# Expert layer of a four-block transformer chain: from all eight experts on every token to tokens sorted by expert, two jobs at a time

## The chip, the cores and the metric

The kernel runs on one core of a Trainium2 chip. The metric is the device time of one execution in microseconds (us). The kernel before takes 533.73 us, the median of three runs (532.73 to 534.79).

## What is computed

The input x is 16 sequences of 128 tokens with 128 features; a context of 16 sequences of 77 tokens goes with it. Four residual blocks follow each other: a cross attention without projections (A), a 16-head self attention whose projection matrices are mixed per sequence from 4 experts (B), a 16-head cross attention with rotary embedding (C), and a causal 16-head self attention that ends in a mixture of experts (D). Only the last one is touched by the change:

```python
y = x + layernorm(attn, ln1_g, ln1_b)
flat = y.reshape(-1, d)
logits = flat @ gate_W                      # 8 experts
topv, topi = jax.lax.top_k(logits, K)       # K = 2
w = jax.nn.softmax(topv, axis=-1)
combine = jnp.sum(jax.nn.one_hot(topi, E) * w[..., None], axis=1)
h = jax.nn.relu(jnp.einsum('nd,edf->enf', flat, W1) + b1[:, None, :])   # 128 -> 512
eo = jnp.einsum('enf,efd->end', h, W2) + b2[:, None, :]                 # 512 -> 128
moe = jnp.einsum('ne,end->nd', combine, eo)
out = y + layernorm(moe.reshape(b, t, d), ln2_g, ln2_b)
```

All eight experts are evaluated for every token in the formula, but only the two with the largest gate logits have a weight that isn't zero.

## The kernel before

Two sequences (`SPS = 2`, 256 tokens, `W`) are one job; there are 8 jobs. Four lanes run side by side, lane s taking jobs s and s + 4. A lane is a list of 68 small steps (`way`): transposes, projections, scores, exponentials, normalisations of the blocks A to D, up to the gate. A fifth lane (`MOE = 4`) takes the jobs in turn through the experts: `moe_start`, 16 pieces `moe` (`PIECES`), `moe_end`, `moe_out`, `store`. A sixth (`PRE = 5`) splits W1 into two half-precision parts in 8 steps.

All engines walk through the same list `STEPS`, which comes from the string `ORDER` (one digit for the lane of each of the 712 steps). Each engine does in this order what is its part of a step, and waits there on semaphores; nothing overtakes on an engine. `TAKEN` gives the PSUM bank of each step. The digits 0 to 3 of job 0's first pass reach its gate (`top`, step 194 of the list, the 187th of the lane steps) before the first digit 4 (step 200).

A `moe` piece on TensorE is two hidden blocks of 128 rows. Each is three half-precision matmuls of 256 columns (lines 659 to 661: W1hi with yhi, W1hi with ylo, W1lo with yhi), then ScalarE's relu with bias (line 804) into `hT`, and with a delay of one piece the second layer in fp32 (line 611: two token blocks for each of two hidden blocks). After each expert VectorE adds the result times the token's weight to `acc` (`take_up`, line 934). `moe_start` puts the combination with b2 into `acc` (line 649), for which `comb` was transposed (`D.cT`, line 539). `moe_end` ends in the moments of `acc`; GpSimd turns them into a scale and a shift (`scales`, lines 1036 to 1039), ScalarE normalises (line 743), GpSimd multiplies and adds (lines 1105, 1108), SyncE stores (line 439).

GpSimd also makes the scales of the lanes' own norms (`ln1`), five in each job. SyncE issues all DMAs: the inputs, the constants, W1 (`w1f`) and W2 (`w2f`) once at the start, whole, and the outputs. `w1f` is overwritten with the probabilities of the attentions (`probs`) once W1 is split, so the first exponential (step `E`) waits for the end of the split.

Of the kernel before, what the change touches and what calls it, by code (L numbers as in the profile page):

```python
# [8 lines left out]
F32 = mybir.dt.float32  # L9
F16 = mybir.dt.float16  # L10
ALU = mybir.AluOpType
# [7 lines left out]
MOE = LANES  # L19
PRE = LANES + 1  # L20
SPLITS = 8
SPS = 2
W = SPS * T
JOBS = B // SPS
CH = FF // 128
UNITS = E1 * CH
# [14 lines left out]
        ("b1", UNITS), ("cos", T), ("sin", T), ("triL1", SPS * E1 * E1), ("triU1", SPS * E1 * E1))  # L41
# [13 lines left out]
HALF = (("ident16", 128), ("lowS", 32), ("lowST", 32), ("spreadS", 96 + T), ("spreadST", 96 + T), ("pick", len(PARTS) * 128), ("two", NT * T))  # L55
HALF_AT, HALF_W = {}, 0
for _n, _w in HALF:
# [7 lines left out]
         "D.xT", "D.qk", "D.v", "D.mt", "D.pv", "D.pt", "D.yT", "D.lg", "D.cT")  # L65
# [4 lines left out]
BANKS, RING, HRING = 8, 8, 4  # L70
STACK_DVE = (1,)
PIECES = UNITS // 2


def way(lane):
# [13 lines left out]
    if lane == PRE:  # L89
        return [("split", lane, n) for n in range(SPLITS)]  # L90
    if lane == MOE:
        return ([("moe_start", lane)] + [("moe", lane, n) for n in range(PIECES)]
                + [("moe_end", lane), ("moe_out", lane), ("store", lane)])
# [8 lines left out]
            + [("y", lane)] + hops("D.yT", "D.lg") + [("top", lane, "D")] + hops("D.cT"))  # L102
# [4 lines left out]
    "0100212001033011011020150202130512032155503012303300220532505321003213100321012002020022023003200223"  # L107
    "0112201203213031100321021020232010310010132001101230132101230130132310031320130230020301102321030201"
    "4414011304124312114014021213042130412041332113241034310223034103124312413430423134234012214044110320"
    "4142101420123244112342104241332410222410134203344321033203122144423102144403414303140340132101430242"  # L110
    "1013042003234013243120342102140113412441320012413103142304032244003342144230012024310430110224013214"
    "0341232423201341012342130023114010243101300441023421033410403214344423442314342142324232412431242131"
    "4321433412434432142134444322433243242442434244344242234444334424434334443434443443444443434444444444"
    "444444444444"
# [17 lines left out]
def uses(step):  # L132
# [4 lines left out]
    if kind == "moe":  # L137
        return 1 + step[2] % 2
# [5 lines left out]
def rounds(lane):  # L144

    return 1 if lane == PRE else JOBS if lane == MOE else len(range(lane, JOBS, LANES))

# [1049 lines left out]
```

## Time and profile before

| | |
|---|---|
| median of the runs | 533.73 us |
| the profiled execution: time / span from first to last instruction | 535.21 / 533.4 us |
| TensorE matmul busy | 471.8 us (88%) |
| ScalarE busy | 371.4 us (70%) |
| VectorE busy | 310.1 us (58%) |
| GpSimd busy | 156.9 us (29%) |
| mean granted TensorE clock | 0.954 |
| mean DMA rate over the span | 20 GB/s |

PE is TensorE's matmul stream, PEld its weight loads, ACT ScalarE, DVE VectorE, POOL GpSimd, SP SyncE (SPq its queue). Matmuls are pipelined: a matmul's own duration includes its passage through the array, so the rate is read from starts, not from durations. "Idle before" is the time that the engine sat idle ahead of an instruction, with what released it. A table by stretches shows in which part of the run an engine is the limit.

### The profile page before, as it was taken

Reading aid. Unit: us, or ns where it says so; the run is one execution under the profiler, and the core shown is the slowest. Engines: PE = TensorE matmul, PEld = TensorE weight load, DVE = VectorE, ACT = ScalarE, POOL = GpSimd, SP = SyncE. Lnnn points to the kernel's source line nnn. Section 1 sums busy time; section 2 is a strip of 40 time slices with the busy share of each in tenths; the row PEclk is TensorE's granted clock in tenths of the full one; section 3 lists DMA queues with packets and bytes.
Section 4 is the critical chain, followed back from the end, with each engine's and each line's share of the span. In section 5 each row is a group of like instructions: output and inputs, shape, how many; then the busy total and the mean of one; then the engine's idle time right before and its main releaser. Section 6 shows DMA issues by size and latency. Waiting matters only on the chain.

```text
span 533.4 us, 18187 instructions
## 1 busy us (share of the span) xinstructions
PE 471.8 (88%) x7456; PEld 385.9 (72%) x7456; DVE 310.1 (58%) x940; ACT 371.4 (70%) x914; POOL 156.9 (29%) x397
## 2 busy tenths in 40 slices
PE   4576777777799999999999999999999999999894
PEld 3344545554578787888887877887778878889793
DVE  3368578558436658775576868575753737232211
ACT  4566655776757787888888878878777785665452
POOL 5425121320241214454462213201331441242302
PEclk9995978999759999999999999999999999999998
DMA  7900000000000000000000000000000000000000
GB/s 238 370 21 17 1 1 3 3 1 4 2 1 2 3 4 1 14 3 1 2 12 2 2 2 14 2 2 3 3 13 2 1 12 3 2 11 1 11 2 10
DMA packets 6776, 10.75 MB, mean 20 GB/s; under 512 B 464, under 2 KB 6056, under 8 KB 6312
## 3 DMA queue, kind: packets, MB, share of 16 engines
q1 hardware_dynamic: 6696, 9.60, 5.2%
q8 instruction: 60, 0.98, 0.8%
q14 instruction: 20, 0.16, 0.1%
HBM read 8.55 MB, written 1.05 MB: 18 GB/s over the span
## 4 chain that ended last, share of the span: by engine, by line
PE 70%; DVE 11%; ACT 7%; issue 4%; POOL 4%; DMA 3%; SPq 1%; POOLq 0%; DVEq 0%; ACTq 0%
PE bk L611 20%; PE bk L601 8%; PE bk L659 5%; DVE negmax L1003 5%; PE bk L660 5%; PE bk L661 5%; PE bk L587 3%; ACT w1f L778 3%; DMA w1f<-in_w 3%; PE bk L580 2%; PE bk L557 2%; PE bk L458 2%; PE bk L520 2%; PE bk L573 2%; PE bk L506 2%
## 5 line engine op out<-in xcount | busy, mean ns | idle before, releaser
L611 PE MATMUL bk<-w2f,hT 128*128 128x128 f32 x1024 | 135.6, 276 | 1.8 <-ACT hT L804 1.8
L804 ACT ACTIVATE hT<-bk,pk 128x256 f32<-128x256 f32 x256 | 107.1, 476 | 37.9 <-PE bk L661 37.3
L611 PEld LDWEIGHTS bk<-w2f,hT 128*128 128x128 f32 x1024 | 124.4, 192 | 4.7 <-ACT hT L804 2.0
L778 ACT ACTIVATE w1f<-bk 128x512 f32<-128x512 f32 (+1 forms) x192 | 98.5, 602 | 26.1 <-PE bk L587 25.7
L1003 DVE TENSOR_REDUCE negmax<-bk 128x4 f32<-128x512 f32 (+1 forms) x192 | 104.9, 611 | 16.3 <-PE bk L587 15.7
L934 DVE SCALAR_TENSOR_TENSOR acc<-bk,comb,acc 128x128 f32<-128x128 f32 x128 | 38.8, 345 | 71.9 <-PE bk L611 71.6
L659 PE MATMUL bk<-yhi,w1hi 128*128 128x256 f16 x256 | 70.7, 276 | 0.0
L661 PE MATMUL bk<-yhi,w1lo 128*128 128x256 f16 x256 | 70.4, 275 | 0.0
L660 PE MATMUL bk<-ylo,w1hi 128*128 128x256 f16 x256 | 70.4, 275 | 0.0
L1036 POOL TENSOR_SCALAR shift<-mv 128x2 f32<-128x2 f32 x40 | 10.0, 251 | 190.0 <-DVE mv L944 189.2
L601 PE MATMUL bk<-w1f,val 128*32 128x128 f32 (+1 forms) x1536 | 55.5, 290 | 1.3 <-ACT w1f L778 1.2
L587 PE MATMUL bk<-qk 32*128 32x128 f16 (+2 forms) x1536 | 46.5, 217 | 5.9 <-ACT w1f L778 2.3
L601 PEld LDWEIGHTS bk<-w1f,val 128*32 128x32 f32 (+1 forms) x1536 | 42.1, 115 | 10.0 <-issue 4.1
L587 PEld LDWEIGHTS bk<-qk 32*128 32x128 f16 (+1 forms) x1536 | 32.6, 99 | 14.3 <-issue 8.3
L764 ACT ACTIVATE qk<-bk 128x512 f16<-128x512 f32 x72 | 37.9, 603 | 4.2 <-PE bk L557 3.8
L659 PEld LDWEIGHTS bk<-yhi,w1hi 128*128 128x128 f16 x256 | 25.6, 100 | 6.8 <-issue 2.2
L580 PE MATMUL bk<-mT,hf 32*128 32x128 f16 (+1 forms) x768 | 28.8, 224 | 1.9 <-ACT w1f L778 0.6
L1038 POOL TENSOR_TENSOR rstd<-ve,neghalf 128x2 f32<-128x2 f32 x40 | 28.4, 711 | 3.3
L580 PEld LDWEIGHTS bk<-mT,hf 32*128 32x128 f16 (+1 forms) x768 | 20.2, 102 | 11.7 <-issue 11.1
L1047 POOL TENSOR_TENSOR pair<-lg 128x16 f32<-128x16 f32 (+1 forms) x32 | 7.7, 263 | 68.2 <-DVE lg L829 49.6
L660 PEld LDWEIGHTS bk<-ylo,w1hi 128*128 128x128 f16 x256 | 25.2, 99 | 3.3
L661 PEld LDWEIGHTS bk<-yhi,w1lo 128*128 128x128 f16 x256 | 25.2, 99 | 3.1
(152 smaller groups left out, 780.3 us busy)
## 6 DMA issues: line engine op xcount, KB each, us to landing
w1f<-in_w SPq DMA_DIRECT2D x1, 2048.0 KB, 14.8
w2f<-in_w SPq DMA_DIRECT2D x1, 2048.0 KB
pk<-in_pack SPq DMA_DIRECT2D x1, 1690.0 KB, 7.8
xin<-in_x SPq DMA_DIRECT2D x8, 128.0 KB, 2.4
out<-outb SPq DMA_DIRECT2D x8, 128.0 KB, 1.8
cin<-in_ctx SPq DMA_DIRECT2D x8, 77.0 KB
hf<-in_half SPq DMA_DIRECT2D x1, 416.0 KB, 10.4
rw<-in_rows SPq DMA_DIRECT2D x1, 320.0 KB, 8.4
```

Of the source, the lines that this page charges most:

```text
L580: mm(banks[q][0:nk, t * T:(t + 1) * T], H("two")[rows_, t * T:t * T + nk], mT[s][rows_, i * T:(i + 1) * T], start=L != "D", stop=False)
L587: last = mm(o, qs if q_first else ks, ks if q_first else qs, start=q_first and L != "D", stop=L != "D" or t == NT - 1)
L601: last = mm(o[32 * t:32 * t + 32, (2 * i + a) * T:(2 * i + a + 1) * T], val[s][0:nk, m, SHIFT * r:SHIFT * r + 32], probs[0:nk, ring(n, q), ...
L611: last = mm(o[:, i * D:(i + 1) * D], hT[:, k % HRING, i * T:(i + 1) * T], w2f[:, k, :], start=c == 0 and i == 0, stop=c == CH - 1, skip_gr ...
L659: mm(o[:, m * W:(m + 1) * W], hi, yhi[s][:], start=True, stop=False)
L660: mm(o[:, m * W:(m + 1) * W], hi, ylo[s][:], start=False, stop=False)
L661: last = mm(o[:, m * W:(m + 1) * W], lo, yhi[s][:], start=False, stop=True)
L764: act.activation(qk[s][:, :, t, :], bank(g, st, t)[:].rearrange("p (n w) -> p n w", n=2), ACT.Copy).then_inc(s_stk_act, 1)
L778: act.activation(probs[0:nk, ring(n, q), :], bank(g, st, q)[0:nk, :], ACT.Exp, scale=SCALE[L]).then_inc(s_exp, 1)
L804: act.activation(hT[:, k % HRING, :], bank(g, st)[:, m * W:(m + 1) * W], ACT.Relu, bias=P("b1")[:, k:k + 1]).then_inc(s_relu, 1)
L934: last = dve.scalar_tensor_tensor(out=acc[:, i, :], in0=products(j, e)[:, i * D:(i + 1) * D], scalar=comb[j % LANES][:, i, e:e + 1], in1=a ...
L1003: dve.tensor_reduce(negmax[s][:, i, NT * q:NT * (q + 1)], bank(g, st, q)[:, 0:NT * nk].rearrange("p (t k) -> p t k", t=NT), X_AXIS, ALU.ma ...
```

## The change

W1 is no longer split and no weights stay on the core. After two jobs (a chunk of `CHUNKS`, 512 tokens, 1024 chosen rows) have passed the gate, the new lane `ROUTE` counts the tokens of each expert (VectorE `choices`, TensorE `count`, VectorE `places`) and gives each chosen row a place in a list sorted by expert, in which every expert begins at a multiple of 128. GpSimd scatters the rows of y there, in memory (`tokens`), with one indirect DMA for each block of 128 tokens and each of the two choices, 4 for a job. The lane `MOE` takes the list in tiles of 128 rows, always 15 for a chunk, 60 in all: SyncE brings the rows (64 KB) and fetches the weights of the one expert (a number read from the chip's memory, 592 KB); TensorE transposes (`turn`), multiplies in fp32 with W1 (`up`) and with W2 (`down`); the result goes to memory (`results`). The lane `OUT` gathers for each job the two result rows of each token (4 indirect DMAs), adds them by weight, and goes on as before. `probs` has memory of its own. The lanes lose `D.cT`, and ylo and yhi go. `ORDER` and `TAKEN` are new: 764 steps, 536 of them of the lanes. The gate of job 0 (`top`) is step 199, `count` of the first chunk 261, the first `turn` 283, which 279 lane steps precede; `count` of the second chunk 402, of the third 595, with the next `turn` at 440 and 617; the last `top` is step 692, `count` of the fourth chunk 697; from the end of `down` 44 (699) on, no lane step is left: `route` 700, `scatter` 701 and 702, `turn` 45 at 703.

```diff
+CHUNKS = ((0, 1), (2, 3), (4, 5), (6, 7))
+MOE, ROUTE, OUT = range(LANES, LANES + 3)
+TILES = [(TOPK * T * n + E1 * 127) // 128 for n in TOK]
+STAGES, ROWRING, OUTRING, GBRING = 4, 3, 3, 2
+EXPERT = (("w1", FF), ("w2", FF), ("b2", D), ("b1", CH))
...
+    if lane == ROUTE:
+        return [st for c, jobs in enumerate(CHUNKS)
+                for st in [("count", lane, c), ("route", lane, c)] + [("scatter", lane, j) for j in jobs]]
     if lane == MOE:
...
+            steps += [("turn", lane, a), ("up", lane, a)]
+            for m in range(a + 1, a + n):
+                steps += [("turn", lane, m), ("up", lane, m), ("down", lane, m - 1)]
+            steps += [("down", lane, a + n - 1)]
+        return steps
+    if lane == OUT:
+        return [(kind, lane, j) for j in OUTS for kind in ("gather", "sum", "moe_out", "store")]
...
-        w1hi = sb("w1hi", [128, UNITS * 128], F16)
-        w1lo = sb("w1lo", [128, UNITS * 128], F16)
-        w2f = sb("w2f", [128, UNITS, D])
+        probs = sb("probs", [128, RING, NT * T])
+        staged = sb("staged", [128, STAGES, EXPERT_W])
...
+            for c in range(len(CHUNKS)):
+                sp.dma_start(tokens[c].rearrange("(n p) d -> p n d", p=128),
+                             zeros[:].unsqueeze(1).to_broadcast((128, TILES[c], D))).then_inc(s_cleared[c], 16)
+            def fetch(m):
+                c, i = TILE[m]
+                if m >= STAGES:
+                    sp.wait_ge(s_down, m - STAGES + 1)
+                    sp.wait_ge(s_tile, m - STAGES + 1)
+                e = sp.value_load(exc[c][0:1, i:i + 1], min_val=0, max_val=E1 - 1)
+                sp.dma_start(staged[:, m % STAGES, :],
+                             experts[bass.DynSlice(e, 1), :, :].rearrange("e p w -> p (e w)")
+                             ).then_inc(s_staged[m % STAGES], 16)
+            def bring(m):
+                c, i = TILE[m]
+                if m >= ROWRING:
+                    sp.wait_ge(s_turn, m - ROWRING + 1)
+                sp.dma_start(rowsT[:, m % ROWRING, :], tokens[c][i * 128:(i + 1) * 128]
+                             ).then_inc(s_rows[m % ROWRING], 16)
...
+                elif kind == "scatter":
+                    c, p = JOB_AT[st[2]]
+                    if p == len(CHUNKS[c]) - 1:
+                        sp.wait_ge(s_scat[c], all_scattered(c))
+                        for m in range(FIRST[c], FIRST[c] + ROWRING):
+                            bring(m)
...
+                elif kind == "turn":
+                    m = st[2]
                     o = take_bank(pe, g, st)
...
+                    pe.wait_ge(s_rows[m % ROWRING], 16 * (m // ROWRING + 1))
+                    pe.transpose(o[:, 0:128], rowsT[:, m % ROWRING, :], ident).then_inc(s_turn, 1)
+                elif kind == "up":
+                    m = st[2]
+                    o = take_bank(pe, g, st)
+                    pe.wait_ge(s_sorted, m + 1)
+                    pe.wait_ge(s_staged[m % STAGES], 16 * (m // STAGES + 1))
+                    for k in range(CH):
+                        last = mm(o[:, k * 128:(k + 1) * 128], expert(m, "w1")[:, k * 128:(k + 1) * 128],
+                                  sorted_[:, m % 2, :], start=True, stop=True)
...
+                elif kind == "down":
+                    m = st[2]
+                    o = take_bank(pe, g, st)
+                    for k in range(CH):
+                        pe.wait_ge(s_relu, CH * m + k + 1)
+                        last = mm(o[:, 0:D], hT[:, m % 2, k * 128:(k + 1) * 128],
+                                  expert(m, "w2")[:, k * D:(k + 1) * D], start=k == 0, stop=k == CH - 1)
...
+                elif kind == "scatter":
+                    j = st[2]
+                    c, p = JOB_AT[j]
+                    pool.wait_ge(s_idx, c + 1)
+                    pool.wait_ge(s_cleared[c], 16)
+                    pool.wait_ge(s_y[j % LANES], j // LANES + 1)
+                    for i in range(SPS):
+                        for k in range(TOPK):
+                            at = (p * SPS + i) * TOPK + k
+                            pool.indirect_dma_start(tokens[c], bass.IndirectOffsetOnAxis(idxc[c][:, at:at + 1], 0),
+                                                    y[j % LANES][:, i, :], None).then_inc(s_scat[c], 16)
+                elif kind == "gather":
+                    j, n = st[2], NUMBER[g, st]
+                    c, p = JOB_AT[j]
+                    for r in range(OUTRING):
+                        stored = len(range(r, FIRST[c] + TILES[c], OUTRING))
+                        pool.wait_ge(s_result[r], 16 * stored)
+                    after(pool, s_mvF, n - GBRING + 1)
```

`choices` is some 7 small operations of VectorE (the ranks that `pick` now leaves in `rankc`, compared with 2, 0 and 1, and the weights of the two choices); `places` is 13, each of which waits for the one before; the places of the rows are ready after the ninth, the experts of the tiles after the last. `take_up` is four operations on 128 columns, after the gathers.

## Rows read from the trace of the kernel before

**Rows 1.** The page, busy time of each engine over the span.

```profile
PE 471.8 (88%) x7456; PEld 385.9 (72%) x7456; DVE 310.1 (58%) x940; ACT 371.4 (70%) x914; POOL 156.9 (29%) x397
```

**Rows 2.** Stretches: length, busy of PE, PEld, DVE, ACT, POOL, clock, DMA share, GB/s.

```profile
0.00:20.00 20.00, 9.47 (x34) 6.52 (x35) 6.86 (x36) 9.34 (x30) 9.47 (x29) 1.00 0.86 305
20.00:110.00 90.00, 64.92 (x1016) 45.64 (x1020) 59.53 (x168) 55.60 (x138) 26.11 (x73) 0.87 0.08 29
110.00:155.00 45.00, 35.89 (x798) 24.93 (x788) 27.87 (x76) 32.65 (x74) 9.22 (x22) 0.83 0.01 3
155.00:500.00 345.00, 337.11 (x5405) 285.78 (x5404) 210.24 (x642) 258.50 (x639) 106.54 (x264) 0.99 0.02 5
500.00:533.40 33.40, 24.47 (x220) 23.02 (x217) 5.61 (x20) 15.32 (x37) 5.57 (x10) 0.93 0.03 9
```

**Rows 3.** Groups by line: busy us, mean ns of one, idle before and releaser.

```profile
L804 ACT ACTIVATE hT<-bk,pk 128x256 f32<-128x256 f32 x256 | 107.1, 476 | 37.9 <-PE bk L661 37.3
L1003 DVE TENSOR_REDUCE negmax<-bk 128x4 f32<-128x512 f32 (+1 forms) x192 | 104.9, 611 | 16.3 <-PE bk L587 15.7
L778 ACT ACTIVATE w1f<-bk 128x512 f32<-128x512 f32 (+1 forms) x192 | 98.5, 602 | 26.1 <-PE bk L587 25.7
L934 DVE SCALAR_TENSOR_TENSOR acc<-bk,comb,acc 128x128 f32<-128x128 f32 x128 | 38.8, 345 | 71.9 <-PE bk L611 71.6
```

**Rows 4.** TensorE in order of time, 470 to 500 us: start, duration, instruction.

```profile
473.09 0.60 PE L520 MATMUL bk<-pk,po 128*128 128x128 f32 x4
473.52 0.27 PE L659 MATMUL bk<-yhi,w1hi 128*128 128x256 f16 x1
...
475.07 0.27 PE L659 MATMUL bk<-yhi,w1hi 128*128 128x256 f16 x1
...
475.73 1.06 PE L611 MATMUL bk<-w2f,hT 128*128 128x128 f32 x8
476.62 0.27 PE L659 MATMUL bk<-yhi,w1hi 128*128 128x256 f16 x1
```

**Rows 5.** Line 864, `comb` of the eight jobs, first and last start.

```profile
L864 DVE TENSOR_TENSOR comb<-picked,lmax x8: 174/175/597, 151.1 to 495.9; 128x16 f32<-128x16 f32 x8
```

**Rows 6.** VectorE in order of time: the small dependent operations of the gate.

```profile
494.96 0.28 DVE L841 TENSOR_REDUCE rank<-pair 128x16 f32<-128x128 f32 x1
...
495.89 0.17 DVE L864 TENSOR_TENSOR comb<-picked,lmax 128x16 f32<-128x16 f32 x1
```

**Rows 7.** All engines in order of time, 524 to 534 us: the end.

```profile
525.53 0.61 DVE L934 SCALAR_TENSOR_TENSOR acc<-bk,comb,acc 128x128 f32<-128x128 f32 x2 [1.83 <-PE bk L611]
...
527.03 0.24 POOL L1036 TENSOR_SCALAR shiftF<-mvF 128x2 f32<-128x2 f32 x1 [24.11 <-DVE mvF L944]
...
528.65 0.88 ACT L743 ACTIVATE zF<-acc,shiftF,rstdF 128x128 f32<-128x128 f32 x2 [4.07 <-POOL shiftF L1039]
529.61 0.72 POOL L1105 TENSOR_TENSOR zgF<-zF,rw 128x256 f32<-128x256 f32 x1 [0.99 <-ACT zF L743]
...
531.22 0.37 SPq L439 DMA_DIRECT2D out<-outb  x1
```

**Rows 8.** DMA issues: KB each and median us from issue to landing.

```profile
w1f<-in_w SPq DMA_DIRECT2D x1, 2048.0 KB, 14.8
...
xin<-in_x SPq DMA_DIRECT2D x8, 128.0 KB, 2.4
out<-outb SPq DMA_DIRECT2D x8, 128.0 KB, 1.8
```

**Rows 9.** SyncE's issue of the second weight matrix: start and duration.

```profile
7.41 2.00 SPq L428 DMA_DIRECT2D w2f<-in_w  x1
```

**Rows 10.** Groups by line again: the split, and two evictions of VectorE.

```profile
L769 ACT ACTIVATE w1hi<-w1f 128x512 f16<-128x512 f32 x8 | 4.8, 622 | 1.5 <-DMA w1f<-in_w 1.5
...
L829 DVE COPY lg<-bk 128x16 f32<-128x16 f32 x8 | 1.3, 166 | 6.6 <-PE bk L534 6.6
L921 DVE TENSOR_TENSOR xs<-bk,xs 128x256 f32<-128x256 f32 x16 | 6.8, 422 | 10.2 <-PE bk L526 10.1
```

More of the change, by code:

```diff
@@ L10 @@
 F16 = mybir.dt.float16
+I32 = mybir.dt.int32
+U32 = mybir.dt.uint32
 ALU = mybir.AluOpType
@@ L136, in uses @@
         return NQ
-    if kind == "moe":
-        return 1 + step[2] % 2
     if step[2:] == ("B.mix",):
         return SPS
-    return int(kind in ("hop", "moe_start") or kind == "PV" and step[3] == 0)
+    return int(kind in ("hop", "count", "turn", "up", "down") or kind == "PV" and step[3] == 0)
 def rounds(lane):
-    return 1 if lane == PRE else JOBS if lane == MOE else len(range(lane, JOBS, LANES))
+    return 1 if lane >= LANES else len(range(lane, JOBS, LANES))
 def schedule():
-    ways, at = [way(lane) for lane in range(PRE + 1)], [0] * (PRE + 1)
+    ways, at = [way(lane) for lane in range(OUT + 1)], [0] * (OUT + 1)
     steps, counts, number, taken, last = [], {}, {}, {}, {}
@@ L167, in schedule @@
     assert next(banks, None) is None
-    assert all(at[lane] == len(ways[lane]) * rounds(lane) for lane in range(PRE + 1))
+    assert all(at[lane] == len(ways[lane]) * rounds(lane) for lane in range(OUT + 1))
     return steps, number, taken
@@ L174, with build @@
 N_CONST = 3
-N_MOE = 2
 FIRST_GATE = next(x for x in STEPS if x[1][2:] == ("B.hid",))
 FIRST_MIX = next(x for x in STEPS if x[1][2:] == ("B.mix",))
-def build(nc, x, ctx, pack, rows, half, w1, w2, b2, out):
+def build(nc, x, ctx, pack, rows, half, experts, out):
     with ExitStack() as stack:
@@ L535, in hop_step @@
                                   start=True, stop=True)
-                elif h == "D.cT":
-                    pe.wait_ge(s_comb[s], g + 1)
-                    for i in range(SPS):
-                        last = pe.transpose(o[0:E1, i * T:(i + 1) * T], comb[s][:, i, :], ident)
                 last.then_inc(s_hop[s], 1)
@@ L604, in weighted @@
                 last.then_inc(s_pv, 1)
-            def down(j, k):
-                e, c = divmod(k, CH)
-                o = take_bank(pe, j, ("moe", MOE, 2 * e + 1), 1) if c == 0 else products(j, e)
-                pe.wait_ge(s_relu, j * UNITS + k + 1)
-                for i in range(SPS):
-                    last = mm(o[:, i * D:(i + 1) * D], hT[:, k % HRING, i * T:(i + 1) * T], w2f[:, k, :],
-                              start=c == 0 and i == 0, stop=c == CH - 1, skip_group_check=True)
-                last.then_inc(s_down, 1)
             pe.wait_ge(s_first, 16)
@@ L1179 @@
             "bo": a["L0_ffn_bo"]}
+    expert = {"w1": a["L1_ffn_W1"], "w2": a["L1_ffn_W2"].reshape(E1, CH, 128, D).transpose(0, 2, 1, 3).reshape(E1, 128, FF),
+              "b2": np.tile(a["L1_ffn_b2"][:, None, :], (1, 128, 1)),
+              "b1": a["L1_ffn_b1"].reshape(E1, CH, 128).transpose(0, 2, 1)}
     arrays = {
@@ L1184 @@
         "half": np.concatenate([half[n].astype(np.float16) for n, _ in HALF], 1),
-        "w1": a["L1_ffn_W1"].transpose(1, 0, 2).reshape(D, -1),
-        "w2": a["L1_ffn_W2"].reshape(UNITS, 128, D).transpose(1, 0, 2),
-        "b2": a["L1_ffn_b2"],
+        "experts": np.concatenate([expert[n] for n, _ in EXPERT], 2),
     }
```

394 lines of the change are left out of this document (244 added, 150 removed).

## The prediction

> **What bounds the kernel now.** I read the page's busy line first: TensorE is busy 88% of the span, ScalarE 70% [rows 1]. That is an average, so the table by stretches comes next [rows 2]. It shows three regimes. From 20 to 155 us only the lanes run (job 0 reaches its gate at 151.1 us [rows 5]), and no engine is full: TensorE is busy 101 of 135 us at a granted clock of 0.83 to 0.87, ScalarE 88, VectorE 87. Here four lanes of dependent steps set the pace. From 155 to 500 us the expert pieces fill every hole: TensorE is busy 337.1 of 345 us at clock 0.99, ScalarE 75%, VectorE 61%. Here TensorE's work is the time. From 500 us on, the last job's experts run alone. So removed TensorE work pays one for one only in the middle regime, and only as long as TensorE stays the limit there.
>
> In order of time, one expert piece repeats every 1.55 us (475.07 to 476.62): six half-precision matmuls of 256 columns in 0.66 us, and four fp32 products of 128 columns (8 records) in 0.89 us, 0.223 each [rows 4]. A job is 16 pieces, 24.8 us, and 0.5 us for b2 and the transposed weights, my estimate: 25.3.
>
> The attention work follows: 337.1 minus 7 jobs of 25.3 is 160 us for the 352 lane steps left after step 200 of 544, 5.2 jobs: 31 us of TensorE per job at full clock. ScalarE's and VectorE's attention work per job is as large: 98.5 us of exponentials and 104.9 us of maxima are only their largest parts [rows 3]; in all (371.4 - 107.1 - 10)/8 = 32 us and (310.1 - 38.8 - 7)/8 = 33 us, where the 10 and the 7 are the split and the small experts' copies, estimated from its 4.8 us [rows 10]. Three equally loaded engines explain why the lanes alone fill none.
>
> **The change part by part.** I build the new time in four stretches: to the first tile, to the last `comb`, and the tail in two parts.
>
> *One tile on TensorE.* `up` and `down` are four fp32 products each, 2 x 0.89 = 1.79 us; the transpose is a quarter of the four that took 473.52 - 473.09 = 0.43 us, 0.11 [rows 4]. Together 1.90 us, 60 tiles 114 us, where 8 jobs of 25.3 were 202. The padding is in this: 1024 rows would fill 8 tiles, and 15 are always run.
>
> *Stretch 1, to the first `turn`.* Now 187 lane steps end at 151.1 us [rows 5]. The removed split took 4.8 us of ScalarE and a wait of 1.5 [rows 10]; VectorE's half is like it. I give back 5 us: 146. But the first tile comes after 279 lane steps, not 187, since two jobs must pass the gate and be sorted. These 92 steps have no expert work beside them. With the first 20 us taken as start-up, about 24 steps by the list, the other 163 take 131 us, 0.80 us a step: 74 us, so 220. By TensorE's work the 92 steps are 1.37 jobs of 31 us, 43 us, which at 75% busy take 57: 203. I take 212 and keep both ends. Clearing the lists (3.9 MB) stands behind the inputs in SyncE's queue, takes the place of the 4 MB of W1 and W2, and is needed first at the first scatter: nothing; without that cover it would cost some 15 us, like `w1f` [rows 8].
>
> *Stretch 2, to the last `comb`.* TensorE's work is 257 lane steps, 3.84 jobs x 31 = 119, and 43 tiles x 1.90 = 82: 201 us. At today's 98% [rows 2] it would be 205. But the lanes alone, at 0.80 us a step, need 206, and the filler has shrunk from 53% of TensorE's work (177 of 337) to 41%. I put the busy share between the regime without filler (75%) and the one with it (98%), at 90 to 91%: 222 us. Upper end 245 (82%): after steps 402 and 595, TensorE has only lane steps until the new list is in place (17 us, next), the second time 18 steps, some 14 us. VectorE gains three routings of about 5 us and two operations a tile, and loses `take_up`'s 39 [rows 3]; ScalarE's relus become four of 128 columns, no longer in all than the 107 us they take [rows 3]. Both stay under TensorE. GpSimd gains 24 scatters and 16 gathers in this stretch, behind which the scales of the lanes' norms queue.
>
> So the last `comb` comes at 212 + 222 = 434 us, where it is at 495.9 now [rows 5]: 62 us gained.
>
> *Tail, routing.* After the last `top` TensorE still has two `up` and three `down`, with two waits, 6 us. VectorE reaches `places` only behind the bias add of `down` 44. Then all is in series: the add 0.3; nine dependent small operations, 0.24 us each by the five in (495.89 + 0.17 - 494.96) = 1.1 us [rows 6], 2.2; eight scatters on GpSimd; landing 2.1, between 1.8 and 2.4 [rows 8]; issue and landing of the first rows 2.6; semaphores 0.5. An indirect DMA on GpSimd is nowhere in the trace. Its issue is bounded by SyncE's fastest, 0.37 us [rows 7], and its slowest, 2.00 us for a transfer of 2 MB [rows 9]. I take 1.2, the middle, as it has to read 128 indices but moves 64 KB. That is 9.6, the gap 17.3 us (11 to 24), with TensorE idle.
>
> *Tail, 15 tiles.* With nothing between them, `up` waits for its own transpose: passage 0.28, VectorE's copy of 128 columns 0.28 (between 0.166 for 16 and 0.422 for 256 with two inputs [rows 10]), semaphores 0.1: 0.66. Period 0.66 + 1.79 = 2.44 us, 15 of them and the last relu and `down` 1.3: 37.9. The fetch of tile m + 4 is issued after `down` m, which leaves 5.8 us until `up` m + 4; it needs about 0.35 + 0.6 + 3.7 us (2 us and 592 KB at some 340 GB/s, between the 305 over the first 20 us [rows 2] and what it would be alone). That fits by 1 us only; upper end 45.
>
> *Tail, out.* Add, issue and landing of the last result: 2.5. Then for job 6 and, since GpSimd takes the gathers of job 7 behind job 6's last addition, again for job 7: four gathers 4.8, landing 2.1, four additions 1.0, moments 0.8, scales 1.65 (527.03 to 528.65), normalise 0.95, two GpSimd operations 1.6 (529.61 to 531.22) [rows 7]: 12.9, twice 25.8. Store 2.2. Together 30.5 (25 to 37.5), where now 7.9 us follow the last products (525.5 to 533.4).
>
> The tail is 6 + 17.3 + 37.9 + 30.5 = 92 us (79 to 112), now 533.4 - 495.9 = 37.5: 54.5 us lost. The sum is 533.4 - 62 + 54.5 = 526 us of span. The profiled execution's 535.2 us lie 1.5 above the median 533.7, its span by chance just below it; I apply the difference of -7.5 to the median: 526 us.
>
> *A rule beside the row.* The nearest row for an indirect DMA is SyncE's issue, 0.37 to 2.00 us [rows 7, 9]; no row shows GpSimd making descriptors. The Trainium skill (SBUF — State Buffer, "Who interferes with whom") speaks against the change: such descriptors are written through a port that some VectorE copies hold, and a transfer of 620 ns alone took 3100 ns beside one. No row here shows it. By it the issue in the busy stretches would grow by the length of a VectorE operation, and in the tail hardly, as VectorE is idle there; it is an addition to the second rival's mechanism below and changes none of its numbers.
>
> **The rivals.**
>
> *TensorE stays full (faster).* If the new order interleaves as well as the old, stretch 2 is 205 us and stretch 1 207: 526 - 17 - 5 = 504 us. For it: 98% today, over 345 us [rows 2]. Against it: less filler, and 80% of that needs the lanes at their own best pace.
>
> *The indirect DMAs are dear (slower).* One mechanism, on GpSimd's queue: at 2.0 us or more each, the 8 scatters and 8 gathers of the tail add 16 x 0.8 = 13 us, and in stretch 2 forty others hold up the lanes' norm scales behind them, 32 us more of GpSimd time, of which a third passes through: 10. That gives 549; at 2.5 us 565. From about 1.6 us each on (16 x 0.4 = 6.4 and 40 x 0.4 / 3 = 5) the change is a loss. For it: 29% busy GpSimd has had no such work, and every job's norms pass it.
>
> *The last tiles run slower.* If the fetch takes 5.8 us or more, or the clock falls to the 0.83 of the stretch 110:155 [rows 2], as TensorE has a hole in every tile, the period is 2.9 us: +7, so 533, no change. The clock was 0.99 where TensorE was full and 0.83 to 0.87 where it was 75% busy; in the tail it would be about 75% busy.
>
> *It doesn't do what it says.* The dense work is 8 x 2048 token rows; sorted it is not the 4096 chosen but 60 x 128 = 7680, as the empty tiles run too. This is certain, and in the sum; it is why 202 us become 114 and not 60.
>
> **How the numbers follow.** A measurement tells about 0.5% from no change, so faster is below 531.1 us, slower above 536.4. Chances: my forecast 0.38 (own range 515 to 538; faster 0.20, same 0.10, slower 0.08); TensorE full 0.22, all faster; dear indirect DMAs 0.27 (same 0.02, slower 0.25); slower last tiles 0.08 (half same, half slower); a mishap in my favour, a shorter first stretch and a short tail, 0.05. Faster 0.47, same 0.16, slower 0.37. The range takes both neighbours in: from 495 (504 less a tail with cheap indirect DMAs) to 565.
>
> **What the profile after would show.** Right: TensorE busy about 385 us; the first fp32 `up` at about 212 us; a hole of some 17 us in TensorE ahead of the last 15 tiles, at about 440 us; a period of 2.44 us in them; 30 us from the last `down` to the end. Wrong if the first tile comes much earlier than 200 us, if TensorE's share between is at 97%, if GpSimd's issues are far from 1.2 us, or if the hole is half or twice as long.

## The result and the profile after

The changed kernel takes 594.9 us (median of four runs, 590.4 to 595.0), the kernel before 533.4 in the same comparison: ratio 1.113, 95% interval [1.107, 1.119]. The forecast was 526 us, its range 495 to 565. It is slower, and outside the range.

The page first: busy time of each engine, and the granted TensorE clock in the 40 slices of the span.

```profile
PE 435.3 (73%) x6668; PEld 335.9 (57%) x6668; DVE 317.2 (53%) x1016; ACT 327.7 (55%) x874; POOL 215.8 (36%) x454
...
PEclk9975979978769757999965899999858999589955
```

TensorE is busy 73% of the span, not 88% [rows 1], and 435 us, not the 385 announced. In the second half of the row of clocks stand slices of 0.5 where TensorE was to be kept full.

Then the stretches, cut at the forecast's own landmarks: first `comb`, first `turn`, last `comb`, first tile of the last 15, last `down`, end. Columns as in [rows 2].

```profile
0.00:159.40 159.40, 114.14 (x1924) 80.73 (x1928) 95.86 (x288) 97.54 (x242) 45.68 (x128) 0.87 0.18 54
159.40:225.20 65.80, 54.07 (x864) 34.72 (x856) 39.65 (x123) 34.63 (x87) 26.39 (x57) 0.68 0.15 49
225.20:494.90 269.70, 228.77 (x3606) 185.99 (x3601) 162.07 (x523) 173.51 (x474) 107.08 (x220) 0.89 0.40 122
494.90:515.20 20.30, 3.35 (x34) 3.05 (x33) 4.88 (x22) 1.47 (x6) 12.45 (x14) 0.67 0.49 164
515.20:558.80 43.60, 34.96 (x255) 31.45 (x255) 10.79 (x45) 17.91 (x62) 8.55 (x15) 0.92 0.66 202
558.80:593.10 34.30, 0.03 (x1) 0.00 (x0) 3.95 (x17) 2.63 (x6) 15.63 (x24) 0.56 0.11 31
```

Against the sum of the prediction (526 as 212, 222, 23.3, 37.9, 30.5): the tail is 98.2 us for 92, the first stretch 225 for 212, and the middle 269.7 for 222. The 48 us of the middle are the surprise.

The places are found by cutting the middle where GpSimd issues indirect DMAs. These are four of those bursts (8, 8, 4 and 8 DMAs), same columns:

```profile
205.14:215.22 10.08, 6.27 (x86) 2.40 (x71) 3.62 (x8) 2.43 (x8) 7.95 (x8) 0.65 0.76 255
301.86:311.83 9.97, 3.48 (x54) 2.24 (x53) 1.75 (x5) 1.65 (x4) 7.83 (x8) 0.67 0.27 85
365.64:370.53 4.89, 2.93 (x63) 1.64 (x62) 2.40 (x6) 1.78 (x6) 3.97 (x4) 1.00 0.72 214
420.97:430.93 9.96, 2.72 (x54) 1.86 (x52) 1.03 (x3) 2.34 (x5) 7.82 (x8) 0.79 0.77 262
```

In them TensorE executes 5 to 13 matmul records per microsecond; over 225.2 to 292.3 us it has 944 in 67.1 us, 14. VectorE and ScalarE stand nearly still too. In order of time, TensorE in the first burst (start, duration, instruction, idle before and releaser):

```profile
209.84 0.78 PE L694 MATMUL bk<-probs,val 128*32 128x128 f32 x6
210.95 0.62 PE L694 MATMUL bk<-probs,val 128*32 128x128 f32 x2 [0.33 <-issue]
212.37 1.08 PE L694 MATMUL bk<-probs,val 128*32 128x128 f32 x4 [0.80 <-issue]
213.78 1.09 PE L694 MATMUL bk<-probs,val 128*32 128x128 f32 x4 [0.34 <-issue]
215.23 1.09 PE L694 MATMUL bk<-probs,val 128*32 128x128 f32 x4 [0.35 <-issue]
```

These are independent products of one step, of which 32 take 1.08 us at 418.11. Here four come every 1.4 us, and between them TensorE waits for nothing that the profile shows ("issue"). The clock is granted at 0.50 from 210 us on. VectorE does not merely wait for TensorE's slow products. Its next maximum needs only the scores of these 16 matmuls, which have ended at 209.90 us, and it starts 6.8 us later, behind a releaser that the profile can't name ("remote"):

```profile
209.29 0.61 PE L680 MATMUL bk<-qk 32*128 32x128 f16 x16
216.75 2.48 DVE L1139 TENSOR_REDUCE negmax<-bk 128x4 f32<-128x512 f32 x4 [6.78 <-remote]
```

So TensorE and VectorE are each held up by themselves, and the lanes stop. On GpSimd itself nothing is strange: an indirect DMA of a burst is issued in 0.96 us with 0.30 between two, 1.26 in all, near the 1.2 of the forecast.

### The profile page after: what moved, and what is told of

Read it like the earlier page. It is cut to its first block, busy times and chain, and to the rows that moved or that the text cites. A ratio compares the mean times of both kernels' runs of the same rounds, so it can differ in the third digit from the quotient of the medians.

```text
span 593.1 us, 17358 instructions
## 1 busy us (share of the span) xinstructions
PE 435.3 (73%) x6668; PEld 335.9 (57%) x6668; DVE 317.2 (53%) x1016; ACT 327.7 (55%) x874; POOL 215.8 (36%) x454
## 4 chain that ended last, share of the span: by engine, by line
PE 50%; DVE 14%; ACT 11%; issue 9%; another core or an unknown queue 5%; POOL 5%; DMA 3%; SPq 1%; POOLq 0%; DVEq 0%; ACTq 0%
PE bk L750 9%; PE bk L758 7%; PE bk L694 7%; DVE negmax L1139 6%; ACT probs L862 5%; PE bk L680 4%; PE bk L673 2%; PE bk L555 2%; PE bk L650 2%; DMA got<-results,idxc 2%; PE bk L568 2%; POOL got L1264 2%; PE bk L666 2%; PE bk L617 1%
## 5 line engine op out<-in xcount | busy, mean ns | idle before, releaser
L862 ACT ACTIVATE probs<-bk 128x512 f32<-128x512 f32 (+1 forms) x192 | 98.4, 600 | 31.9 <-PE bk L680 27.7
L883 ACT ACTIVATE hT<-bk,staged 128x128 f32<-128x128 f32 x240 | 68.8, 375 | 61.1 <-PE bk L750 40.8
L750 PE MATMUL bk<-sorted,staged 128*128 128x128 f32 x480 | 73.7, 301 | 13.0 <-ACT hT L883 3.7
L750 PEld LDWEIGHTS bk<-sorted,staged 128*128 128x128 f32 x480 | 63.8, 206 | 22.0 <-ACT hT L883 10.0
L694 PE MATMUL bk<-probs,val 128*32 128x128 f32 (+1 forms) x1536 | 63.0, 298 | 9.5 <-ACT probs L862 4.8
L758 PE MATMUL bk<-staged,hT 128*128 128x128 f32 x480 | 65.2, 280 | 0.0
L758 PEld LDWEIGHTS bk<-staged,hT 128*128 128x128 f32 x480 | 59.4, 195 | 1.1 <-issue 0.4
L694 PEld LDWEIGHTS bk<-probs,val 128*32 128x32 f32 (+1 forms) x1536 | 44.5, 118 | 23.0 <-issue 13.0
L1252 POOL DMA_INDIRECT tokens<-y,idxc x32 | 31.6, 986 | 21.8 <-DVE idxc L1048 13.0
L1264 POOL DMA_INDIRECT got<-results,idxc x32 | 31.4, 983 | 9.4 <-issue 9.4
L743 PE MATMUL bk<-pk,rowsT 128*128 128x128 f32 x60 | 18.1, 301 | 16.2 <-DMA rowsT<-tokens 16.2
L1132 DVE CAST qk<-bk 128x512 f16<-128x512 f32 x24 | 16.4, 684 | 23.3 <-remote 16.4
```

Source lines behind the costliest of these rows:

```text
L694: last = mm(o[32 * t:32 * t + 32, (2 * i + a) * T:(2 * i + a + 1) * T], val[s][0:nk, m, SHIFT * r:SHIFT * r + 32], probs[0:nk, ring(n, q), ...
L750: last = mm(o[:, k * 128:(k + 1) * 128], expert(m, "w1")[:, k * 128:(k + 1) * 128], sorted_[:, m % 2, :], start=True, stop=True)
L758: last = mm(o[:, 0:D], hT[:, m % 2, k * 128:(k + 1) * 128], expert(m, "w2")[:, k * D:(k + 1) * D], start=k == 0, stop=k == CH - 1)
L862: act.activation(probs[0:nk, ring(n, q), :], bank(g, st, q)[0:nk, :], ACT.Exp, scale=SCALE[L]).then_inc(s_exp, 1)
L883: act.activation(hT[:, m % 2, k * 128:(k + 1) * 128], bank(g, st)[:, k * 128:(k + 1) * 128], ACT.Relu, bias=expert(m, "b1")[:, k:k + 1]).t ...
L1252: pool.indirect_dma_start(tokens[c], bass.IndirectOffsetOnAxis(idxc[c][:, at:at + 1], 0), y[j % LANES][:, i, :], None).then_inc(s_scat[c], 16)
```

## The experiments

Four theories. **A**: while GpSimd prepares an indirect DMA, the instruction stream and the signals of the other engines arrive late. **B**: the bursts of four weight fetches (592 KB each) do it, as they start together with many of these bursts. **C**: GpSimd's in-order queue, the forecast's second rival: what stands behind the DMAs is late. **D**: the lanes' own pace in the new order. Names: `b_` kernels add something to the kernel before, `a_` kernels alter the changed one. Each is timed beside the kernel before (533.2 to 534.3 us in these comparisons).

**Theory A, alone, on the kernel before.** Four operations at expert piece 8 (of 0 to 15) of each of the eight jobs. `b_ind` has

```diff
+                elif kind == "moe" and st[2] == 8:
...
+                    for k in range(4):
+                        pool.indirect_dma_start(junk[:, k, :], None, x.rearrange("b t d -> (b t) d"),
+                                                bass.IndirectOffsetOnAxis(idl[:, k:k + 1], 0)).then_inc(s_junk, 16)
```

> The kernel before (533.4 us) with 32 indirect gathers of 64 KB more on GpSimd, four at the eighth expert piece of each of the eight jobs; nobody waits for them but the end. Theory A (while GpSimd prepares the descriptors of an indirect DMA, the instruction stream and the signals of the other engines arrive late): 8 bursts of about 5 us in which TensorE gets half of its work or less, so 20 to 35 us slower, with holes in TensorE's timeline in every burst. Theory B (the bursts of weight fetches starve the core): within 3 us of before. Theory C (what stands behind the indirect DMAs on GpSimd's queue, the lanes' norm scales, comes late): up to 8 times 5 us, the same as the kernel with busy GpSimd of equal length. Theory D (the lanes' own pace): no change.

`b_busy` has an addition of 128x448 in place of each, which took 1.15 us:

> The kernel before with 32 additions of 128x448 on GpSimd (an estimated 1.0 to 1.3 us each, from the 0.96 us of an indirect DMA and the busy groups of GpSimd) at the same places as the 32 indirect gathers; they touch data of nobody. Theory A: under 5 us slower, since no descriptors are made. Theory C: as much slower as with the indirect gathers (20 us or more). B and D: no change.

`b_dir` has `pool.dma_start(junk[:, k, :], x[2 * g + k % 2])`:

> The kernel before with 32 plain DMAs of 64 KB, issued by GpSimd at the same places. Theory A in its wide form (any descriptor making on GpSimd starves the others): as slow as the indirect gathers, 20 to 35 us. In its narrow form (indirect ones alone): within 3 us of before. B: within 3 us.

and `b_sp` the same line on SyncE:

> The kernel before with 32 plain DMAs of 64 KB, issued by SyncE at the same places: the same bytes, no work on GpSimd. All of A, C and D: within 2 us of before. B (DMA traffic as such): a few us slower.

Measured: `b_ind` 536.6 us, ratio 1.007 [1.004, 1.009]; `b_busy` 534.4, 1.002 [1.000, 1.005]; `b_dir` 533.5, 1.001 [0.999, 1.003]; `b_sp` 533.2, 0.998 [0.995, 1.002]. The indirect ones cost 3.0 us, where theory A said 20 to 35, and no burst is starved. The first of them:

```profile
179.37:184.35 4.98, 4.94 (x168) 3.71 (x164) 0.59 (x1) 4.57 (x10) 4.07 (x4) 1.00 0.16 42
```

168 matmul records in 5 us beside four indirect DMAs. So theory A as stated falls: making indirect descriptors does not by itself starve anybody. C has nothing for it either: GpSimd's 1.15-us additions in the same places cost nothing that can be told.

**The changed kernel, one part at a time.** `a_small` fetches only 128 of the 1156 columns of an expert after the first four tiles, so it leaves out most of the expert weights:

```diff
+                w = EXPERT_W if m < STAGES else 128
-                sp.dma_start(staged[:, m % STAGES, :],
-                             experts[bass.DynSlice(e, 1), :, :].rearrange("e p w -> p (e w)")
+                sp.dma_start(staged[:, m % STAGES, 0:w],
+                             experts[bass.DynSlice(e, 1), :, 0:w].rearrange("e p w -> p (e w)")
```

> The changed kernel (594.9 us) with each fetch of a tile's expert after the first four cut to 128 of its columns, so most expert weights are left out. Theory B (bursts of four weight fetches starve the core): 30 us or more faster than the changed kernel. Theory A (indirect DMAs on GpSimd starve it): under 8 us faster, and the holes in TensorE's timeline during the scatters and gathers stay. C and D: under 8 us.

`a_dirpool` makes each of the 64 indirect DMAs a plain one of as many bytes, to and from fixed rows. It leaves out the sorting:

```diff
-                            pool.indirect_dma_start(tokens[c], bass.IndirectOffsetOnAxis(idxc[c][:, at:at + 1], 0),
-                                                    y[j % LANES][:, i, :], None).then_inc(s_scat[c], 16)
+                            pool.dma_start(tokens[c][at * 128:(at + 1) * 128], y[j % LANES][:, i, :]).then_inc(s_scat[c], 16)
...
+                            pool.dma_start(got[:, n % GBRING, i, k, :], results[c][at * 128:(at + 1) * 128]).then_inc(s_got[n % GBRING], 16)
```

> The changed kernel with its 64 indirect DMAs as plain DMAs of the same bytes to fixed rows, still issued by GpSimd; the tokens are not sorted. Theory A, narrow (indirect ones alone): 40 to 55 us faster than the changed kernel, near 545 us. Theory A, wide (any descriptor making on GpSimd): under 15 us faster. B: no gain. C: no gain if the plain ones hold GpSimd as long.

`a_sp` issues those plain DMAs on SyncE, with the same waits in front of them:

> The changed kernel with its 64 indirect DMAs as plain DMAs of the same bytes to fixed rows, issued by SyncE; GpSimd issues none, the tokens are not sorted. Theory A (both forms) and C: 40 to 55 us faster than the changed kernel, near 545 us, and no holes at the scatters. B: under 10 us faster, and holes stay where the weight fetches are. D: under 10 us.

and `a_sp_small` has the small fetches of `a_small` as well:

> As the one with plain DMAs on SyncE, and with the fetches of the experts cut to 128 columns as well (most expert weights left out). What it gains over that one is the price of the fetches: A says under 6 us, B 30 us or more.

Measured: `a_small` 592.7 us; `a_dirpool` 546.7; `a_sp` 561.3; `a_sp_small` 551.1 (against the kernel before 1.111 [1.107, 1.116], 1.026 [1.021, 1.031], 1.054 [1.048, 1.061], 1.036 [1.029, 1.042]). B falls: without five sixths of the fetched weight bytes the changed kernel gains 2 us. D falls: with the same order of steps it gains 48 us when the DMAs are plain, and the last `comb` moves from 494.9 to 453.9 us. That `a_sp` is 15 us behind `a_dirpool`, though GpSimd is freer, and that small fetches give back some 10 of them, fits SyncE's queue having become the place where fetches and scatters wait for one another; this was not followed further.

So the indirect form is needed for the loss, and yet harmless on the kernel before. What differs?

**Which of them, and is it their memory?** `a_gind` leaves only the gathers indirect, `a_sind` only the scatters:

> The changed kernel with its 32 scatters as plain DMAs to fixed rows (GpSimd still issues them, tokens not sorted), its 32 gathers still indirect. All 64 plain took 546.7 us and all 64 indirect 594.9. If the scatters alone starve the core: near 547 plus 32 times the longer issue of a gather where it is waited for, 547 to 553. If each indirect DMA costs the same: near 570. If it is the gathers: near 590.

> The changed kernel with its 32 gathers as plain DMAs from fixed rows, its 32 scatters still indirect. If the scatters starve the core: 585 to 592 us. If each indirect DMA costs the same: near 570. If it is the gathers: 550 or less.

`b_scat` and `b_gscr` repeat `b_ind` with scatters to, and gathers from, shuffled rows of a scratch tensor in memory:

```diff
+                        pool.indirect_dma_start(scratch, bass.IndirectOffsetOnAxis(idl[:, k:k + 1], 0),
+                                                junk[:, k, :], None).then_inc(s_junk, 16)
```

> The kernel before with 32 indirect scatters of 64 KB from SBUF to shuffled rows of a scratch tensor in memory, at the places where 32 indirect gathers cost 3.6 us. If indirect writes starve the core: 20 us slower or more, with TensorE's rate of instructions halved in each burst. If what starves the core is particular to the changed kernel: 2 to 5 us, as with the gathers.

> The kernel before with 32 indirect gathers at the same places, now from shuffled rows of a scratch tensor in memory in place of evenly spaced rows of the input. If the source or the order of the rows is what starves the changed kernel: 15 us slower or more. Else 2 to 5 us, as with the first gathers.

Measured: `a_gind` 555.0 us, 1.044 [1.040, 1.047]; `a_sind` 555.1, 1.041 [1.037, 1.045]; `b_scat` 538.7, 1.010 [1.006, 1.013]; `b_gscr` 537.1, 1.008 [1.006, 1.011]. None of the three expectations for the pair holds: with none indirect 546.7, with either half 555, with both 594.9. 8 and 8 do not make 48. And the first burst of scatters shows it already, before any gather is executed. Here it is in `a_sind` (the same eight scatters, the same steps beside them as in the burst at 205.14 above):

```profile
203.24:213.80 10.56, 8.26 (x182) 5.47 (x186) 9.73 (x24) 5.68 (x15) 8.42 (x8) 0.84 0.77 266
```

182 matmul records where the changed kernel has 86, and 24 VectorE instructions where it has 8. Up to this point both have executed the same work; they differ in what the program holds later. This leaves two properties of the whole program: both forms in it, or their number.

**Form or number.** `a_half` keeps half of the scatters and half of the gathers indirect (both forms, 32 in number); the second sequence of each job goes unsorted:

```diff
+                            if i == 0:
                                 pool.indirect_dma_start(...)
+                            else:
+                                pool.dma_start(spare[(2 * j + k) * 128:(2 * j + k + 1) * 128], y[j % LANES][:, i, :])
```

> The changed kernel with half of its scatters and half of its gathers as plain DMAs of GpSimd (to a spare tensor, from the input; the second sequence of each job goes unsorted), the other 16 scatters and 16 gathers indirect: both forms, 32 indirect DMAs in all. If it is the presence of both forms that costs: 575 us or more. If it is the number of indirect DMAs in the program (32 of either form alone gave 555): near 555.

`b_g64` is `b_gscr` with eight gathers in each place, 64; `b_both` has four scatters and four gathers in each:

> The kernel before with 64 indirect gathers in place of 32 (eight at each place), one form only. If the number counts: 20 us slower than before or more, with TensorE's records halved in each burst of 10 us. If each costs its own: 6 to 10 us slower (twice the 3.8 us of 32). If both forms together count: 6 to 10 us too.

> The kernel before with 32 indirect scatters and 32 indirect gathers (four and four at each place). If both forms in one program, or 64 in number, starve the other engines: 20 us slower or more, with TensorE's records halved. If each costs its own: 8 to 10 us (5.4 and 3.8 measured alone). If it takes something else of the changed kernel: 8 to 10 us too.

Measured: `a_half` 560.4 us, 1.049 [1.045, 1.053]; `b_g64` 606.8, 1.137 [1.134, 1.140]; `b_both` 604.4, 1.134 [1.130, 1.139]. Both forms together at 32 cost 13.7 us over plain, 5 more than either form alone, but not the 48 of 64. The number is what costs: the kernel before, which has no sorting, no expert fetch and no new order, becomes 73.6 us slower with 64 dummy gathers of one form that nobody waits for. Its TensorE shows the same picture (kernel `b_g64`, its second burst in four slices of 2.5 us, columns as in [rows 2]):

```profile
250.30:252.80 2.50, 1.48 (x46) 0.62 (x36) 1.27 (x7) 0.05 (x1) 2.04 (x2) 1.00 0.10 26
252.80:255.30 2.50, 0.85 (x16) 0.44 (x16) 0.00 (x0) 0.00 (x0) 1.90 (x2) 1.00 0.18 52
255.30:257.80 2.50, 1.47 (x8) 0.67 (x9) 0.00 (x0) 0.00 (x0) 1.90 (x2) 0.50 0.20 52
257.80:260.30 2.50, 1.90 (x9) 1.28 (x7) 0.00 (x0) 0.00 (x0) 2.02 (x3) 0.50 0.19 52
```

and TensorE in order of time in the same burst:

```profile
251.54 0.27 PE L596 MATMUL bk<-qk 32*128 32x128 f16 x4 [0.32 <-issue]
252.30 0.26 PE L589 MATMUL bk<-mT,hf 32*128 32x128 f16 x4 [0.49 <-issue]
252.35 0.23 PE L596 MATMUL bk<-qk 32*128 32x128 f16 x2
253.06 0.25 PE L596 MATMUL bk<-qk 32*128 32x128 f16 x2 [0.47 <-issue]
...
258.79 0.37 PE L670 MATMUL bk<-yhi,w1lo 128*128 128x256 f16 x1 [0.39 <-issue]
...
260.24 0.99 PE L620 MATMUL bk<-w2f,hT 128*128 128x128 f32 x3 [0.21 <-issue]
261.65 0.37 PE L620 MATMUL bk<-w2f,hT 128*128 128x128 f32 x1 [0.41 <-issue]
```

A handful of instructions comes every 0.75 us at clock 1.00, and every 1.4 us once the clock is at 0.50. That the interval doubles with the clock suggests that what holds TensorE back goes with TensorE's own clock; no run tests it, and more the trace does not tell. VectorE is held up here too. It has only the transposed weights to copy, which are ready before 257 us, and starts 5 us later:

```profile
256.17 0.59 PE L548 MATMUL bk<-pk,comb 128*8 128x128 f32 x2
261.86 0.41 DVE L937 COPY combT<-bk 8x256 f32<-8x256 f32 x1 [10.15 <-remote]
```

**Where the limit is, and of what.** `b_g48` has six gathers in each place. `b_g64h` has 64 gathers of 64 rows in place of 128. `b_g40` keeps the bursts at four, as in `b_gscr`, but has ten of them:

```diff
-                elif kind == "moe" and st[2] == 8:
+                elif kind == "moe" and (st[2] == 8 or st[2] == 2 and g in (2, 5)):
```

> The kernel before with 48 indirect gathers (six at each place); 32 cost 3.8 us, 64 cost 73.6. If there is a limit in number below 48: about 50 us slower, with TensorE's records halved in each burst of 7.5 us. If the limit lies at 48 or above: 5 to 8 us slower, with the records as in the kernel before. If the cost grows smoothly with the number: about 25 us.

> The kernel before with 64 indirect gathers of 64 rows each in place of 128 (half the rows and bytes: 4096 rows in all, as many as the 32 gathers that cost 3.8 us). If the number of rows (descriptors) counts: 5 to 10 us slower and no starved burst. If the number of indirect DMA instructions counts: 40 us slower or more.

> The kernel before with 40 indirect gathers of 128 rows in ten bursts of four (at the eight places, and two more in the middle of jobs 2 and 5). 32 in bursts of four cost 3.8 us, 48 in bursts of six 47.8. If the limit in number lies at 32: about 40 us slower (ten starved bursts of 4.9 us, as 0.8 of their length was lost with 48), the very first burst starved. If it lies between 40 and 48, or if it is bursts of over four in a row that starve the kernel before: 4 to 7 us slower, with the first burst at over 150 matmul records as with 32.

Measured: `b_g48` 581.1 us, 1.087 [1.078, 1.096]; `b_g64h` 603.0, 1.134 [1.125, 1.143]; `b_g40` 570.5, 1.068 [1.062, 1.074]. Half the rows change little (69.6 us for 73.6), so it is the number of indirect DMA instructions in the program, not of rows or bytes. Bursts of four, which hold GpSimd no longer than those of `b_gscr`, are starved as well once there are ten of them. The same first burst, in `b_gscr` (32 in the program) and in `b_g40` (40):

```profile
179.09:184.08 4.99, 4.95 (x164) 3.55 (x155) 0.69 (x1) 4.64 (x11) 4.08 (x4) 1.00 0.17 42
```

and

```profile
184.37:189.33 4.96, 3.77 (x74) 2.03 (x66) 0.00 (x0) 1.51 (x4) 4.05 (x4) 1.00 0.17 43
246.49:251.36 4.87, 2.37 (x61) 1.11 (x53) 1.31 (x7) 0.09 (x2) 3.95 (x4) 0.97 0.16 40
```

The last line is the next burst of `b_g40`. Not all ten are starved alike, though. These are the last two of `b_gscr`, then the last two of `b_g40`:

```profile
474.97:479.86 4.89, 4.89 (x47) 4.68 (x45) 2.06 (x6) 3.23 (x8) 3.97 (x4) 1.00 0.16 44
500.90:505.79 4.89, 4.89 (x46) 4.67 (x46) 0.61 (x2) 2.46 (x6) 3.97 (x4) 1.00 0.24 67
512.90:517.77 4.87, 4.87 (x47) 4.67 (x45) 1.46 (x4) 3.22 (x8) 3.95 (x4) 1.00 0.17 44
539.00:543.85 4.85, 4.85 (x46) 4.63 (x44) 0.61 (x2) 2.51 (x6) 3.94 (x4) 1.00 0.27 69
```

TensorE is full in all four. (Two more of `b_g40`'s bursts, at 286.90 and 466.49 us, leave it idle for only 0.4 and 0.2 us.) In the four it has only expert pieces, under 10 matmul records per microsecond, where the first burst of `b_gscr` has 33. This fits a limit on how fast instructions reach the engine, but it is no proof. On the kernel before the cost goes 3.8, 36.2, 47.8, 73.6 us for 32, 40, 48, 64: a step between 32 and 40, and from there about 0.9 to 1.15 us for each indirect DMA of the program, 0.74 to 0.93 of the length of its burst. The time of `b_g40` is the one expected for "the limit lies at 32", though fewer than the ten bursts expected are starved; whether the limit is 32 exactly or something up to 39 was not measured, nor why such a limit exists.

## Why the prediction was wrong

Stretch by stretch, in us; "plain" is `a_dirpool`, the same kernel without indirect DMAs:

| | forecast | after | plain |
|---|---|---|---|
| to the first `turn` | 212 | 225.2 | 218.0 |
| to the last `comb` | 222 | 269.7 | 235.9 |
| to the first of the last 15 tiles | 23.3 | 20.3 | 19.3 |
| last 15 tiles | 37.9 | 43.6 | 42.9 |
| out | 30.5 | 34.3 | 27.8 |
| span | 525.7 | 593.1 | 543.9 |

**The step that failed: the indirect DMAs in the busy stretches.** The prediction took them as occupation of GpSimd's queue, 1.2 us each, and let them cost nothing at that price while the lanes pass. The price was right (0.96 us, 1.26 from one to the next). What it did not have is that with 64 in the program TensorE, VectorE and ScalarE are held up while GpSimd issues them (54 matmul records in the 10 us at 301.86, where 140 would be usual); why, no run shows. The runs with one half indirect give 8.4 us each over plain; if these two add, 563 us would be the kernel without that effect, and about 32 us are the effect. By `a_half`, whose 32 cost 13.7 us, twice that would be 27 and the effect 21. Most of it falls on the first two stretches, as the table shows. The second rival named the right instructions and the right side, but on a mechanism that was not at work: GpSimd's queue was not slower than foreseen, and an equally long addition on GpSimd cost nothing that could be told (`b_busy`). Its 549 to 565 us were never a bound for this.

**Stretch 1, mis-sized.** The first tile came at 218.0 in the plain kernel and was forecast at 212, between the ends 203 and 220. From 151.1 us, where job 0's gate was, the 92 added steps took 66.9 us, 0.73 each, or 72 and 0.78 if the split's 5 us were given back. That is the upper end's 0.80 a step, not the 0.62 by TensorE's share: the lanes alone keep their pace per step. (In the plain kernel job 0's gate itself comes at 158.1 us, as 200 lane steps lead to it in the new order; the 79 behind it take 59.9 us, 0.76 each.) The other 7 us, to 225.2, are the starved first burst and the clock of 0.50 in the 10 us behind it: in `a_sind`, with the same eight scatters and no starved burst, the first tile comes at 218.8.

**Stretch 2, share right, work mis-sized.** In the plain kernel TensorE is busy 215.9 of 235.9 us:

```profile
218.00:453.90 235.90, 215.91 (x3601) 177.99 (x3601) 161.01 (x524) 173.05 (x474) 92.98 (x220) 0.96 0.46 140
```

That is 91.5%, for which 90 to 91 was forecast. The work was forecast at 201 us. A tile costs more than 1.90: in the last 15, with little beside them, TensorE is busy 34.56 us in the plain kernel, 2.3 a tile with the start-up at half clock, and 2.65 - 0.52 = 2.1 in a steady one (below). Some 0.2 x 43 tiles is 9 us; the clock of 0.96 for the 0.99 of [rows 2] is 3% of 216, another 6. Together they are the 15 us, the first only as an estimate.

**The count of the DMAs, misplaced.** The prediction put 24 scatters and 16 gathers into this stretch and 8 of each into the tail. By the list of steps the first eight scatters stand before the first `turn`, and the gathers of jobs 4 and 5 among the last 15 tiles. So it is 16 and 16 here, and 8 and 16 in the tail. At 1.2 us each this changes little. In the second rival the stretch would have 32 in place of 40 and the tail 24 in place of 16.

**Tail routing, right.** Last `comb` to the first tile was forecast at 6 + 17.3 us and is 20.3. The hole itself, the nine small operations to `idxc` and the first scatters (VectorE and GpSimd in order of time):

```profile
499.24 0.18 DVE L1030 TENSOR_TENSOR tmp<-bk,pk 128x32 f32<-128x32 f32 x1
...
501.00 0.17 DVE L1048 CAST idxc<-slotk 128x8 uint32<-128x8 f32 x1
...
501.47 1.10 POOL L1252 DMA_INDIRECT tokens<-y,idxc  x1 [4.72 <-DVE idxc L1048]
...
502.88 0.96 POOL L1252 DMA_INDIRECT tokens<-y,idxc  x1 [0.30 <-issue]
...
515.21 0.45 PE L743 MATMUL bk<-pk,rowsT 128*128 128x128 f32 x1 [16.22 <-DMA rowsT<-tokens]
```

The gap is 16.2 us, 17.3 forecast. Eight scatters last to 511.4, 10 us for the 9.6 of the sum; the chain on VectorE is 1.9 for 2.2.

**15 tiles, period 2.65 for 2.44.** TensorE in order of time:

```profile
517.92 0.42 PE L743 MATMUL bk<-pk,rowsT 128*128 128x128 f32 x1
...
522.29 0.27 PE L743 MATMUL bk<-pk,rowsT 128*128 128x128 f32 x1
...
524.94 0.27 PE L743 MATMUL bk<-pk,rowsT 128*128 128x128 f32 x1
525.73 1.13 PE L750 MATMUL bk<-sorted,staged 128*128 128x128 f32 x8 [0.52 <-DVE sorted L1156]
526.70 1.06 PE L758 MATMUL bk<-staged,hT 128*128 128x128 f32 x8
527.59 0.27 PE L743 MATMUL bk<-pk,rowsT 128*128 128x128 f32 x1
```

From the transpose to `up` 0.79 us (525.73 - 524.94), not 0.66, and `up` and `down` 1.86, not 1.79; times 15 this is 3 us. The tile between 517.92 and 522.29 runs at half clock after the hole, 1.7 us more. 43.6 in place of 37.9 is near the upper end of 45. The third rival thus existed as a start-up at half clock, not as a lower clock throughout (0.92 over the stretch), and the fetch that "fits by 1 us" is not what `up` waits for in these tiles.

**Out.** 12.8 us for a job's round (562.19 to 574.97), 12.9 forecast. The stretch is 34.3 us, 30.5 forecast, for two other reasons. Job 6's gathers begin 3.4 us after the last `down`, for 2.5, behind job 5's last addition on GpSimd. And from the issue of the last store to the end it is 5.4 us, where 2.2 were taken from [rows 7]:

```profile
587.65 0.38 SPq L536 DMA_DIRECT2D out<-outb  x1
```

The span ends at 593.1. The plain kernel has the same 5.4 us (538.45 to 543.9); what fills them was not followed.

**TensorE stays full** (504 us) did not come about even in the plain kernel, whose share was 91.5%. **It doesn't do what it says** stayed as in the sum: 60 tiles, 480 records each of L750 and L758.

**The rule of the Trainium skill** (SBUF — State Buffer, "Who interferes with whom") is not what cost the time. By it an indirect DMA beside VectorE's copies would itself take longer. The durations of the 32 of `b_ind` (min/median/max) hardly spread:

```profile
L1110 POOL DMA_INDIRECT junk<-in_x,idl x32: 942/947/1237, 179.4 to 505.5; - x32
```

The maximum is the first of a burst. But only one copy and two casts of VectorE fall beside these 32, so they hardly test the rule. In `a_sind` one scatter in the middle of a burst (at 209.85 us) took 1.42 us, beside a subtraction of VectorE between two tiles (L1122), for a median of 0.96: one in 32, by half a microsecond, and what delayed it is not shown. In the starved bursts it is the other engines that slow down, not GpSimd, and that only beyond some number in the program. A sum made of issue prices can't contain that.

Would the change pay without the effect? The plain kernel does no sorting, and so stands for what the change costs with free addressing: 546.7 us, 2.6% over the kernel before. So of the 61 us lost, some 32 are the effect, some 16 the indirect form itself at 32 or fewer (if the two halves add; 27, and 21 for the effect, by `a_half`), and 13 the structure: 218 us before the first tile, with only the lanes at work, and a tail of 90 us for 37.5. No version that sorts and beats the kernel before was found or tried; one with at most 32 indirect DMAs in all would, by these numbers, still be at about 555 to 563 us.

## What to carry to other kernels

Count the indirect DMAs of a program before sizing them: 32 were nearly free on the kernel before (0.1 to 0.2 us each), 40 and more cost about 1 us each, paid by the other engines, whoever waits for them; only bursts beside few and long matmuls went free. An effect of this kind shows as "issue" idle on TensorE, a few instructions at a time in even intervals, and as waits of VectorE and ScalarE of 5 to 11 us with a releaser "remote". It is told from a queue or traffic effect by adding the suspected operation alone to the kernel before, in the number in which the changed kernel has it; half the number gave the opposite verdict here. And where work is delayed until two jobs are through (a sort, a batch), price the tail first: here it grew from 37.5 to 90 us even without the effect, against 88 us of TensorE work saved by the forecast, and 76 at the 2.1 us that a tile took.

## What the runs showed of the hardware

- An indirect DMA of 128 rows of 512 bytes is issued by GpSimd in 0.94 to 0.96 us, 1.26 from one to the next; with 64 rows its burst of eight takes 9.5 us for 9.9, so the rows hardly count. A plain DMA of the same bytes is 0.56 us on GpSimd.
- With 32 such instructions in a program the other engines are undisturbed (164 and 168 matmul records in the first burst of `b_gscr` and `b_ind`), with 40, 48 and 64 they are held up from the first burst on (74 records in `b_g40`'s first), but not in `b_g40`'s last two, where TensorE has only expert pieces.
- 32 indirect and 32 plain DMAs on GpSimd together take 560.4 us in the changed kernel (`a_half`), 64 plain ones 546.7 (`a_dirpool`), 64 indirect ones 594.9: only the indirect ones count.
- Held up, TensorE gets four to six matmul records every 0.75 us at clock 1.00, about four every 1.4 us at clock 0.50 (`b_g64`); VectorE and ScalarE then start nothing for up to 10 and 11 us.
